# A top-2 mixture of experts behind a gated mLSTM block: seven half-size products for the first expert layer

## The chip, the cores and the metric

The kernel runs on one core of one Trainium2 chip. The metric is the time of one execution on the device in microseconds (us). Three runs of the kernel before gave 1991.71, 1995.03 and 1996.44 us, a median of 1995.03 us. The engines are named as the profile names them: PE (TensorE, the matrix products), DVE (VectorE), ACT (ScalarE), POOL (GpSimd) and SP (the queue that issues plain DMAs).

## The reference, cut to what matters

The program first computes a gated mLSTM attention block over 4096 tokens of width 512, then a feed-forward block of eight experts with two experts for each token. The change touches only the second:

```python
# x: 4096 tokens of width 512; E = 8 experts, K = 2, hidden width H = 2048
gates = softmax(xf @ Wg.T)                # router
topw, topi = top_k(gates, K)
C = int(round(K * T * 1.05 / E))          # 1075 slots an expert
buf = zeros((E, C + 1, D)).at[e_ord, pos].add(x_disp)[:, :C]
h = gelu(einsum('ecd,edh->ech', buf, W1) + b1, approximate=False)
y = einsum('ech,ehd->ecd', h, W2) + b2
out = einsum('tk,tkd->td', cw, y_tk)      # weighted by the router, added to x
```

## The kernel before

The program has two stages. The first 384 us (attention, router, ranks, and the table `slot_row` that says which token sits in which slot of which expert) are nearly untouched by the change. The rest is the stage of the experts.

An expert has `HI = 9` row tiles of `RT = 120` slots, 1080 in all. They are worked in `NC = 3` chunks of 360 slots. For each chunk, the hidden width of 2048 goes in `HT = 16` tiles of 128, so an expert has 48 steps. One step is `first_layer(n + 2)` followed by `second_layer(n)`:

- `first_layer` (L879) makes one hidden tile, 128 x 360, in one of three PSUM banks. The contraction over 512 has four parts. Each part has three products, because every operand is split into a rounded upper part and its rest (`w_hi` x `x_hi`, `w_hi` x `x_lo`, `w_lo` x `x_hi`). That is 12 matmuls with 360 moving columns.
- ACT takes Gelu of it twice (L1135 to `h_raw`, L1136 rounded to `h_hi`), DVE subtracts (L1495, `h_lo`).
- `second_layer` (L892) adds this hidden tile into the three output tiles of the chunk, 120 x 512 each, three products a tile: 9 matmuls with 512 moving columns. An output tile lives in its bank for 16 steps, so PSUM sums the whole hidden width.

After a chunk, DVE adds `b2` (L1511), scales by the router's weight (L1523), and POOL adds the 120 rows to `out` in DRAM by one indirect DMA (L603). There are 9 such adds for an expert, each waiting for the one before. POOL also gathers the token rows of the next chunk (L594) and the router's weights (L609). PE transposes the gathered rows (L862), ACT rounds them (L1060) and DVE makes the rest (L1480). The weights of an expert are split into `w_hi` and `w_lo` (L1070, L1071, L1451, L1453) in the last chunk of the expert before, and stay in place for the whole expert. Each engine has its own program in a fixed order. They meet at semaphores only.

Of the kernel before, what the change touches and what calls it, by code (L numbers as in the profile page):

```python
# [29 lines left out]
NH = 4  # L30
# [12 lines left out]
CT = 3  # L43
NC = HI // CT
CW = CT * RT
assert HI == CT * NC and CW <= 512 and CAP <= HI * RT
PAD = P
# [31 lines left out]
def build(nc, x, ctx_in, g_xattn, g_ffn, w_ig, b_ig, w_fg, b_fg, ln_w, w_router, w1, b1, w2, b2, out):  # L79
# [9 lines left out]
    with stack:  # L89
# [15 lines left out]
        slot_prob = sb("slot_prob", [P, NC, CT, E])  # L105
# [13 lines left out]
        pad_row = sb("pad_row", [P, 1], F32, a_mem)  # L119
        work = sb("work", [P, 2, TT // 2, E], F32, a_mem)  # L120
# [54 lines left out]
        x_hi = sb("x_hi", [P, NC, KT, CW], F32R)  # L175
        x_lo = sb("x_lo", [P, NC, KT, CW], F32R)
        h_raw = sb("h_raw", [P, 3, CW])
        h_hi = sb("h_hi", [P, 3, CW], F32R)
        h_lo = sb("h_lo", [P, 3, CW], F32R)
        y_out = sb("y_out", [P, CT, D])  # L180
# [3 lines left out]
        rows_add = [sb(f"rows_add{t}", [P, 1], I32) for t in range(CT)]  # L184
        rows_turn = sb("rows_turn", [P, HI], I32)
        w_hi = sb("w_hi", [P, HT, 2 * D], F32R)
        w_lo = sb("w_lo", [P, HT, 2 * D], F32R)

        raw = sb("raw", [P, 2, 4 * D])
        gathered = sb("gathered", [P, 3, D])  # L190
# [62 lines left out]
        prob_in = [sem(f"prob_in{c}") for c in range(NC)]  # L253
# [7 lines left out]
        raw_in = [sem(f"raw_in{i}") for i in range(2)]  # L261
        w_upper = sem("w_upper")
        w_ready = sem("w_ready")
        row_in = [sem(f"row_in{i}") for i in range(3)]
        rows_turned = sem("rows_turned")
        x_upper = sem("x_upper")
        x_ready = sem("x_ready")
        h_summed = sem("h_summed")
        h_upper = sem("h_upper")
        h_split = sem("h_split")  # L270
        y_step = sem("y_step")
        y_tile = sem("y_tile")
        y_taken = sem("y_taken")
        y_ready = sem("y_ready")
        y_added = sem("y_added")
        rows_free = sem("rows_free")
        b2_in = sem("b2_in")
        turn_rows_copied = sem("turn_rows_copied")
        b1_copied = sem("b1_copied")
# [3 lines left out]
        N_CONST = 9  # L283

# [42 lines left out]
        EARLY, SOON, LATER = range(0, 2), range(2, 4), range(4, HT)  # L327
# [18 lines left out]
        YB, HB, XB = 0, 3, 6  # L346

        STEPS = NC * HT


        TURN_AT = {c * HT + 7 + 2 * t: CT * c + t for c in range(NC) for t in range(CT)}


        AHEAD = 2

        def turns_of(n, last):
            m = TURN_AT.get(n)
            return [] if m is None or (last and m >= HI - CT) else [m]

        def x_place(m):  # L360

            return (m // CT + 1) % NC, m % CT
# [4 lines left out]
        from_start = [rows_free, y_taken, y_ready, x1_made, xn_made, *x1_stored, back_turned, back_copied, logits_made, logits_copied]  # L367
# [19 lines left out]
        def wait_step(eng, e, n):  # L387

            c, j = divmod(n, HT)
            if j == HT - 1:  # L390
                eng.wait_ge(y_tile, e * HI + CT * (c + 1))
            else:
                eng.wait_ge(y_step, e * (NC * (HT - 1)) + (c * (HT - 1) + j + 1))

        def w_at(j):

            return HT - 1 - j

# [10 lines left out]
        def _(sp):  # L409
# [62 lines left out]
            sp.dma_start(xn_dram[TOK:TOK + PAD, :], zeros[:, :]).then_inc(xn_stored, 16)  # L472
            sp.dma_start(out[TOK:TOK + PAD, :], zeros[:, :]).then_inc(pad_stored, 16)
            sp.dma_start(prob_dram[TOK:TOK + PAD, :], zeros[:, 0:E]).then_inc(prob_stored, 16)
# [9 lines left out]
            def load_weights(e, g, wait):  # L484

                if wait is not None:
                    wait_apart(sp, w_ready, wait)
                sp.dma_start(raw[:, g % 2, 0:2 * D].rearrange("p (k c) -> p k c", k=KT),
                             w1[e].rearrange("(k p) n -> p k n", p=P)[:, :, 2 * g * P:(2 * g + 2) * P]).then_inc(raw_in[g % 2], 16)
                sp.dma_start(raw[:, g % 2, 2 * D:4 * D].rearrange("p (j n) -> p j n", j=2),  # L490
                             w2[e, 2 * g * P:(2 * g + 2) * P, :].rearrange("(j p) n -> p j n", p=P)).then_inc(raw_in[g % 2], 16)
# [4 lines left out]
            for g in range(HT // 2):  # L496
                if g == 2:
                    store_x1(LAST_BATCH)
                    store_xn(LAST_BATCH)
                load_weights(0, g, None if g < 2 else 2 * (g - 1))  # L500
                if g == 3:
                    sp.wait_ge(prob_made, 1)
                    sp.dma_start(prob_dram[0:TOK, :].rearrange("(t p) e -> p t e", p=P), logits[:, :, :]).then_inc(prob_stored, 16)

            def load_b2(e):

                wait_apart(sp, y_taken, START + e * HI)
                sp.dma_start(b2_row[:, :], b2[e].partition_broadcast(P)).then_inc(b2_in, 16)

            with sp.Fori(0, E - 1) as e:  # L510
                load_b2(e)
                for g in range(HT // 2):
                    load_weights(e + 1, g, e * HT + (HT + 2 * (g - 1)))
            load_b2(E - 1)
            sp.wait_ge(y_added, 16 * HI * E)
            for p in range(2):
                sp.wait_ge(x1_stored[p], START + 16 * (B // 2))
            sp.wait_ge(pad_stored, 16)
# [6 lines left out]
        def _(pool):  # L525
# [9 lines left out]
            for p in range(2):  # L535
# [13 lines left out]
                   channel_multiplier=1, allow_small_or_imprecise_dtypes=True)  # L549
            G.iota(pad_row[:, :], pattern=[[0, 1]], base=TOK, channel_multiplier=1,  # L550
# [23 lines left out]
            def first_rests(tiles):  # L574

                for j in tiles:
                    pool.wait_ge(w_upper, j + 1)
                    G.tensor_tensor(w_lo[:, w_at(j), 0:D].rearrange("p (k c) -> p k c", k=KT), raw_w1(j),
                                    w_hi[:, w_at(j), 0:D].bitcast(F32).rearrange("p (k c) -> p k c", k=KT), ALU.subtract)
                    G.tensor_tensor(w_lo[:, w_at(j), D:2 * D], raw_w2(j), w_hi[:, w_at(j), D:2 * D].bitcast(F32), ALU.subtract)\  # L580
                        .then_inc(w_ready, 1)

# [4 lines left out]
            pool.wait_ge(pad_stored, 16)  # L587
# [10 lines left out]
            def add_rows(e, u, ordered=True):  # L598

                wait_apart(pool, y_ready, START + e * HI + (u + 1))  # L600
                if u > 0 and ordered:
                    wait_apart(pool, y_added, e * (16 * HI) + 16 * u)
                G.indirect_dma_start(out=out[:, :], out_offset=bass.IndirectOffsetOnAxis(ap=rows_add[u % CT][0:RT, :], axis=0),  # L603
                                     in_=y_out[0:RT, u % CT, :], in_offset=None, compute_op=ALU.add,
                                     bounds_check=TOK + PAD - 1, oob_is_err=True).then_inc(y_added, 16)
# [968 lines left out]
```

## Time and profile before

| | |
|---|---|
| median of three runs | 1995.03 us |
| the profiled execution | 1997.23 us |
| its span, first to last instruction | 1995.2 us |
| PE busy | 1899.8 us (95%) |
| DVE busy, ACT busy, POOL busy | 752.3 us, 790.7 us, 344.1 us |
| first matmul of an expert | 383.98 us |
| last matmul ends | 1981.4 us |
| moved by DMA | 158.10 MB |

The busy time of an engine is a union: matmuls overlap in the pipeline, so the mean duration of one (328 ns for 360 columns) is not its share of the time. That share is the distance between starts, which the chain and the timeline give.

### The profile page before, as it was taken

What the parts mean: (1) busy time and instruction counts of PE and PEld (TensorE: products, weight loads), DVE (VectorE), ACT (ScalarE), POOL (GpSimd) and SP (SyncE); (2) the same over time, 40 slices, a digit from 0 to 9 for tenths busy, and PEclk for the clock granted to TensorE, in tenths of its full rate; (3) what the DMA queues carried; (4) which work ended last, traced back from release to release, by engine and by line L of the source; (5) the groups of instructions that cost most, each with busy time, mean ns of one, the idle gap of its engine ahead of it and who ended that gap; (6) DMA issues with size and microseconds to landing.
All of it is one profiled execution on the core that took longest, in us unless ns stands there. A gap on an engine that the chain in (4) does not pass through costs nothing.

```text
span 1995.2 us, 28698 instructions
## 1 busy us (share of the span) xinstructions
PE 1899.8 (95%) x10268; PEld 1655.8 (83%) x10268; DVE 752.3 (38%) x1827; ACT 790.7 (40%) x1667; POOL 344.1 (17%) x302
## 2 busy tenths in 40 slices
PE   4999987799999999999999999999999999999997
PEld 3777766688888888888888888888888888888886
DVE  3589987412351235123512351235123512351221
ACT  2567667542352235223522352235223522352221
POOL 0001010262201220122012201220122012201200
PEclk8899987699999999999999999999999999999998
DMA  4255443331241123112311231123212321231111
GB/s 145 85 179 203 163 154 127 96 133 31 64 136 37 31 68 135 34 30 65 134 37 30 62 134 40 30 55 133 48 30 55 132 49 30 57 106 31 31 15 15
DMA packets 111349, 158.10 MB, mean 79 GB/s; under 512 B 13744, under 2 KB 63024, under 8 KB 110208
## 3 DMA queue, kind: packets, MB, share of 16 engines
q1 hardware_dynamic: 92800, 120.68, 18.0%
q0 software_dynamic: 18432, 35.69, 10.2%
q8 instruction: 95, 1.56, 0.3%
q14 instruction: 22, 0.18, 0.0%
HBM read 121.13 MB, written 35.20 MB: 78 GB/s over the span
## 4 chain that ended last, share of the span: by engine, by line
PE 84%; DMA 6%; DVE 4%; issue 3%; ACT 2%; SPq 1%; POOL 0%; POOLq 0%; DVEq 0%; ACTq 0%
PE PS L892 38%; PE PS L879 36%; DMA out_dram<-y_out,rows_add 3%; PE PS L731 3%; PE PS L722 2%; DMA vs<-in_ctx_dram 2%; PE PS L862 2%; PE PS L670 1%; PE PS L750 1%; ACT heads L976 1%; SPq L420 1%; DVE stats L1178 1%; PE PS L684 1%; DMA gathered<-xn_rows,rows_turn 1%; DVE decay L1236 0%
## 5 line engine op out<-in xcount | busy, mean ns | idle before, releaser
L1135 ACT ACTIVATE h_raw<-PS,b_now 128x360 f32<-128x360 f32 x384 | 215.5, 561 | 1035.9 <-PE PS L879 1033.9
L1495 DVE TENSOR_TENSOR h_lo<-h_raw,h_hi 128x360 fp32r<-128x360 f32 x384 | 205.2, 534 | 1074.5 <-ACT h_hi L1136 1073.6
L879 PE MATMUL PS<-x_hi,w_hi 128*128 128x360 f32 x1536 | 503.6, 328 | 2.7 <-issue 1.4
L879 PE MATMUL PS<-x_hi,w_lo 128*128 128x360 f32 x1536 | 503.5, 328 | 0.0
L879 PE MATMUL PS<-x_lo,w_hi 128*128 128x360 f32 x1536 | 501.9, 327 | 0.0
L892 PE MATMUL PS<-w_hi,h_hi 128*120 128x512 f32 x1152 | 459.9, 399 | 0.0
L892 PE MATMUL PS<-w_lo,h_hi 128*120 128x512 f32 x1152 | 453.9, 394 | 0.0
L892 PE MATMUL PS<-w_hi,h_lo 128*120 128x512 f32 x1152 | 453.2, 393 | 0.0
L603 POOL DMA_INDIRECT out_dram<-y_out,rows_add x72 | 129.1, 1793 | 1197.5 <-DVE y_out L1523 986.1
L879 PEld LDWEIGHTS PS<-x_hi,w_hi 128*128 128x128 f32 x1536 | 289.8, 189 | 25.0 <-issue 3.9
L879 PEld LDWEIGHTS PS<-x_lo,w_hi 128*128 128x128 f32 x1536 | 289.3, 188 | 16.4
L879 PEld LDWEIGHTS PS<-x_hi,w_lo 128*128 128x128 f32 x1536 | 289.9, 189 | 0.0
L892 PEld LDWEIGHTS PS<-w_hi,h_lo 128*120 128x120 f32 x1152 | 208.8, 181 | 59.1
L892 PEld LDWEIGHTS PS<-w_hi,h_hi 128*120 128x120 f32 x1152 | 209.2, 182 | 38.4
L892 PEld LDWEIGHTS PS<-w_lo,h_hi 128*120 128x120 f32 x1152 | 208.9, 181 | 38.3
L1136 ACT ACTIVATE h_hi<-PS,b_now 128x360 fp32r<-128x360 f32 x384 | 212.4, 553 | 0.0
L1451 DVE TENSOR_TENSOR w_lo<-raw,w_hi 128x512 fp32r<-128x512 f32 x114 | 78.8, 691 | 45.9 <-ACT w_hi L1071 45.9
L731 PEld LDWEIGHTS PS<-vs,decay 128*128 128x128 f32 x640 | 79.4, 200 | 8.4 <-issue 4.3
L731 PE MATMUL PS<-vs,decay 128*128 128x129 f32 x640 | 83.8, 288 | 0.7 <-DVE decay L1236 0.4
L1071 ACT CAST w_hi<-raw 128x512 fp32r<-128x512 f32 x128 | 80.2, 627 | 0.0
L1070 ACT CAST w_hi<-raw 128x512 fp32r<-128x512 f32 x128 | 79.6, 622 | 0.3
L1453 DVE TENSOR_TENSOR w_lo<-raw,w_hi 128x512 fp32r<-128x512 f32 x114 | 78.1, 685 | 0.0
(177 smaller groups left out, 1432.5 us busy)
## 6 DMA issues: line engine op xcount, KB each, us to landing
raw<-in_L_ffn_W_dram SPq DMA_DIRECT2D x128, 512.0 KB, 4.5
x_front<-in_x_dram SPq DMA_DIRECT2D x8, 1024.0 KB, 7.1
vs<-in_ctx_dram SPq DMA_DIRECT2D x32, 256.0 KB, 4.7
maxima<-maxima_rows SPq DMA_DIRECT2D x8, 1024.0 KB, 4.7
x_back<-in_x_dram SPq DMA_DIRECT2D x8, 1024.0 KB, 8.9
out_dram<-x_back SPq DMA_DIRECT2D x8, 1024.0 KB, 6.9
xn_rows<-xn SPq DMA_DIRECT2D x8, 1024.0 KB, 9.5
b_row<-in_L_ffn_b_dram SPq DMA_DIRECT2D x8, 256.0 KB, 3.6
```

The source lines that it names most:

```text
L603: G.indirect_dma_start(out=out[:, :], out_offset=bass.IndirectOffsetOnAxis(ap=rows_add[u % CT][0:RT, :], axis=0), in_=y_out[0:RT, u % CT, ...
L722: T.matmul(score_ps[t], kT[p][:, h, t * P:(t + 1) * P], qT[p][:, h, t * P:S], start=True, stop=True).then_inc(scores_made, 1)
L731: ins = T.matmul(head_ps[:, s, 0:DH + 1], decay[h % 2][:, t, s * P:(s + 1) * P], vs[p][:, t, h, 0:DH + 1], start=(t == 0), stop=(t == s))
L879: ins = T.matmul(PS[:, HB + n % 3, 0:CW], w[:, w_at(j), k * P:(k + 1) * P], v[:, c, k, :], start=(k == 0 and a == 0), stop=(k == KT - 1 an ...
L892: ins = T.matmul(PS[0:RT, YB + t, :], h[:, n % 3, t * RT:(t + 1) * RT], w[:, w_at(j), D:2 * D], start=(j == 0 and a == 0), stop=(j == HT - ...
L1070: A.copy(w_hi[:, w_at(j), 0:D].rearrange("p (k c) -> p k c", k=KT), raw_w1(j))
L1071: A.copy(w_hi[:, w_at(j), D:2 * D], raw_w2(j)).then_inc(w_upper, 1)
L1135: A.activation(h_raw[:, n % 3, :], PS[:, HB + n % 3, 0:CW], ACT.Gelu, bias=b1_now[:, n % HT:n % HT + 1])
L1136: A.activation(h_hi[:, n % 3, :], PS[:, HB + n % 3, 0:CW], ACT.Gelu, bias=b1_now[:, n % HT:n % HT + 1]).then_inc(h_upper, 1)
L1451: V.tensor_tensor(w_lo[:, w_at(j), 0:D].rearrange("p (k c) -> p k c", k=KT), raw_w1(j), w_hi[:, w_at(j), 0:D].bitcast(F32).rearrange("p (k ...
L1453: V.tensor_tensor(w_lo[:, w_at(j), D:2 * D], raw_w2(j), w_hi[:, w_at(j), D:2 * D].bitcast(F32), ALU.subtract)\
L1495: V.tensor_tensor(h_lo[:, n % 3, :], h_raw[:, n % 3, :], h_hi[:, n % 3, :].bitcast(F32), ALU.subtract)\
```

## The change

The first layer is computed by Winograd's form of Strassen's scheme, on halves. The contraction of 512 is cut in two halves of 256, two hidden tiles of 128 form a pair, and the slots are cut in quarters of `CW = 270`, two of which form a side (540 slots). One `2 x 2` block product then takes seven half-size products instead of eight. An expert has 8 pairs and 2 sides, so 16 blocks (`k` in the code). A block has seven products of 6 matmuls each (2 contraction parts x 3 rests) with 270 moving columns. The operands of the products are sums of weight quarters (`sum_w1`, four DVE operations for a pair) and of token quarters (`sum_x`, four for a side). The results of the seven products, in a ring of four PSUM banks, are combined by one ACT copy and seven DVE adds into `c_top` and `c_rows` in SBUF. Gelu reads them there.

The second layer now runs in groups of four hidden tiles. An output tile is finished after 4 tiles x 3 products = 12 matmuls, taken out, scaled and added to `out` in DRAM. So an expert has 36 adds instead of 9 (288 instead of 72 in all), `y_out` is a ring of three, and an add waits for nothing but its rows. `b2` is added only to the first nine tiles (`base_rows`, DVE). ACT scales all (`scale_rows`). The second layer lags the first by 20 tile steps (`LAG`), across experts.

Unrounded operands and their rests now share one place in SBUF (`same_place`). Weights come in rings of four pairs and are split during the expert, and the pads behind `out` triple.

```diff
-CT = 3
-NC = HI // CT
-CW = CT * RT
+CW = HI * RT // 4
+PAIRS = HT // 2
+RINGS = 3
+PAD = RINGS * P
...
+        PRODUCTS = ((A11, B11), (S2, T2), (S3, T3), (S1, T1), (A22, T4), (S4, B22), (A12, B21))
+        M1, M6, M7, M5, M4, M3, M2 = range(7)
+        U2, U3, C22, U4, C21, C12, C11 = range(1, 8)
+        USED_UP_BY = {M6: U2, M7: U3, M5: U4, M4: C21, M3: C12, M2: C11}
+        LAG = 20
+        def items(k):
+            q = 9 * k - LAG
+            return [[(q + i) for i in range(a, z)] for a, z in ((0, 2), (2, 4), (4, 6), (6, 9))]
+        def scaled_in(k):
+            u = 9 * (k // 4)
+            return ([u - 6, u - 5], [u - 4, u - 3], [u - 2, u - 1], [u, u + 1, u + 2])[k % 4]
...
# POOL
+            def add_rows(e, u):
+                wait_apart(pool, y_ready, e * NY + (u + 1))
+                G.indirect_dma_start(out=out[:, :], ... compute_op=ALU.add, ...).then_inc(y_added[u % RINGS], 16)
...
+                for k in range(BLOCKS):
+                    for u in scaled_in(k):
+                        if not (first and u < 0):
+                            add_rows(e, u)
...
+                    if k == 3 and not last:
...
+                        gather_side(e + 1, 0, rows_turn, True)
+                        wait_apart(pool, weight_copied, e + 1)
+                        gather_prob(rows_turn)
+                    if k == 14 and not last:
+                        gather_side(e + 1, 1, rows_turn, True)
...
# PE
-                for k in range(KT):
-                    for a, (w, v) in enumerate(((w_hi, x_hi), (w_hi, x_lo), (w_lo, x_hi))):
-                        ins = T.matmul(PS[:, HB + n % 3, 0:CW], w[:, w_at(j), k * P:(k + 1) * P], v[:, c, k, :],
+                for kt in range(2):
+                    for n, (w, v) in enumerate(((w1_hi, x_hi), (w1_hi, x_lo), (w1_lo, x_hi))):
+                        ins = T.matmul(product_at(k, i), w[:, slot, a, kt * P:(kt + 1) * P], v[:, side, x, kt, :],
...
+            def second_layer(e, q):
+                g, t, i = q // 36, q % 36 // 4, q % 4
+                u = HI * g + t
...
+                    before = u - 2
+                    if 0 <= before < HI:
+                        pe.wait_ge(y_based, e * HI + (before + 1))
+                    else:
+                        wait_past(pe, y_ready, e * NY + (before + 1))
...
+                    product(e, k, M1)
+                    product(e, k, M6)
+                    rows(0)
+                    rest(0)
+                    rows(1)
+                    product(e, k, M7)
+                    product(e, k, M5)
+                    rows(2)
+                    rest(1)
+                    product(e, k, M4)
+                    rows(3)
+                    rest(2)
+                    rows(4)
+                    product(e, k, M3)
+                    product(e, k, M2)
+                    rest(3)
...
# DVE
+            def base_rows(e, u):
+                dve.wait_ge(y_tile, e * NY + (u + 1))
...
+                wait_past(dve, y_added[u % RINGS], e * (16 * NY // RINGS) + 16 * (u // RINGS))
+                V.tensor_tensor(y_out[0:RT, u % RINGS, :], PS[0:RT, YB + u % 2, :], b2_row[0:RT, :], ALU.add).then_inc(y_based, 1)
```

On PE, at the border between a step's second layer and the next first layer, the order before is this (`h_split` counts the rests that DVE made, `h_upper` the tiles that ACT rounded):

```order
L892 MATMUL PS<-w_hi,h_hi 120x512 [waits h_split]
L892 MATMUL PS<-w_lo,h_hi 120x512
L892 MATMUL PS<-w_hi,h_lo 120x512
...
L879 MATMUL PS<-x_hi,w_hi 128x360 [waits h_upper]
L879 MATMUL PS<-x_lo,w_hi 128x360
L879 MATMUL PS<-x_hi,w_lo 128x360
```

In the changed program, PE at the end of block `k = 5` of an expert, the last product and then the item that closes tile 7 and the one that opens tile 8 (`c_made` counts the DVE adds that empty a bank, `y_based` the output tiles with `b2`):

```order
L958 MATMUL PS<-x_hi,w1_hi 128x270 [waits c_made]
L958 MATMUL PS<-x_lo,w1_hi 128x270
L958 MATMUL PS<-x_hi,w1_lo 128x270
...
L980 MATMUL PS<-w2_hi,h_hi 120x512
L980 MATMUL PS<-w2_lo,h_hi 120x512
L980 MATMUL PS<-w2_hi,h_lo 120x512
L975 REGISTER_ALU
L980 MATMUL PS<-w2_hi,h_hi 120x512 [waits y_based]
```

Each product is a shorter run of matmuls behind a wait of its own, and an output tile opens behind a wait for the tile two before it.

On POOL, an expert of the loop before: the adds stand three at a time, each behind the one before, with three gathers and three weight gathers between:

```order
L594 DMA gathered<-xn_rows,rows_turn 120x512 [waits rows_turned] x3
L609 DMA slot_prob<-prob_rows,rows_turn 120x8 x3
L384 REGISTER_ALU
L384 REGISTER_ALU [waits y_ready]
L603 DMA out_0_dram<-y_out,rows_add0 4224x512 [waits y_added]
```

And in the changed program, block `k = 3` of an expert and the first add of block 4:

```order
L674 DMA out_0_dram<-y_out,rows_now 4480x512 [waits y_ready]
L430 ISA
L430 ISA [waits row_in0,row_in1,row_in2,row_in3,row_in4]
L706 ISA [waits prob_in]
L706 COPY rows_turn<-slot_row 128x9
...
L663 DMA gathered<-xn_rows,rows_turn 120x512 [waits rows_turned] x2
L681 DMA slot_prob<-prob_rows,rows_turn 120x8 [waits weight_copied]
L681 DMA slot_prob<-prob_rows,rows_turn 120x8 x8
L430 REGISTER_ALU
L674 DMA out_0_dram<-y_out,rows_now 4480x512 [waits y_ready]
```

Five row gathers and nine weight gathers of the next expert now stand in one run between two adds.

On DVE, in block `k = 5`, the base of tile 6 stands between two steps of the combination:

```order
L1717 TENSOR_TENSOR c_top<-PS,c_top 128x270 [waits product_made]
L1665 REGISTER_ALU
L1666 REGISTER_ALU [waits w1_summed]
L1667 TENSOR_TENSOR w1_lo<-w1_raw,w1_hi 128x512 [waits w1_upper]
L1708 REGISTER_ALU
L423 REGISTER_ALU [waits y_tile]
L1712 TENSOR_TENSOR y_out<-PS,b2_row 120x512 [waits y_added0]
L1716 REGISTER_ALU
L1717 TENSOR_TENSOR c_rows<-PS,c_rows 128x270 [waits product_made]
```

What DVE had free of waits on DRAM now has a wait for an add (`y_added0`) in the midst of it.

## Rows read from the trace of the kernel before

**Rows 1.** The page: busy time, share of the span, instructions.
```profile
PE 1899.8 (95%) x10268; PEld 1655.8 (83%) x10268; DVE 752.3 (38%) x1827; ACT 790.7 (40%) x1667; POOL 344.1 (17%) x302
```

**Rows 2.** The chain that ended last, near its end: start us, us, what.
```profile
1950.76 2.09 PE PS L892 x9
...
1973.14 1.98 PE PS L879 x12
1975.12 6.28 PE PS L892 x27
```

**Rows 3.** Stretches: us, busy and count of PE, PEld, DVE, ACT, POOL; PEclk, DMA, GB/s.
```profile
200.00:206.00 6.00, 6.00 (x44) 4.77 (x41) 5.19 (x16) 5.37 (x14) 0.29 (x1) 1.00 0.00 0
384.00:390.00 6.00, 6.00 (x22) 6.00 (x23) 0.00 (x0) 1.96 (x3) 3.63 (x5) 0.55 0.77 232
440.00:640.00 200.00, 199.82 (x1051) 177.60 (x1050) 61.95 (x120) 69.95 (x140) 43.76 (x36) 1.00 0.28 72
1220.00:1241.00 21.00, 20.51 (x111) 18.24 (x112) 4.36 (x8) 5.51 (x11) 3.15 (x4) 1.00 0.08 22
```

**Rows 4.** Timeline of PE and its weight loads in the attention stage: start, us.
```profile
202.56 0.75 PEld L700 LDWEIGHTS PS<-g_log,ones 128*128 128x128 f32 x6
204.27 1.95 PE L731 MATMUL PS<-vs,decay 128*128 128x129 f32 x16
```

**Rows 5.** Groups of the page: busy us, mean ns of one, idle before.
```profile
L1495 DVE TENSOR_TENSOR h_lo<-h_raw,h_hi 128x360 fp32r<-128x360 f32 x384 | 205.2, 534 | 1074.5 <-ACT h_hi L1136 1073.6
L1451 DVE TENSOR_TENSOR w_lo<-raw,w_hi 128x512 fp32r<-128x512 f32 x114 | 78.8, 691 | 45.9 <-ACT w_hi L1071 45.9
L731 PE MATMUL PS<-vs,decay 128*128 128x129 f32 x640 | 83.8, 288 | 0.7 <-DVE decay L1236 0.4
```

**Rows 6.** Timeline of DVE and ACT in the expert stage.
```profile
559.99 0.69 DVE L1451 TENSOR_TENSOR w_lo<-raw,w_hi 128x512 fp32r<-128x512 f32 x1 [0.49 <-ACT w_hi L1071]
560.60 0.69 DVE L1453 TENSOR_TENSOR w_lo<-raw,w_hi 128x512 fp32r<-128x512 f32 x1
...
566.45 0.56 ACT L1135 ACTIVATE h_raw<-PS,b_now 128x360 f32<-128x360 f32 x1 [1.97 <-PE PS L879]
566.91 0.55 ACT L1136 ACTIVATE h_hi<-PS,b_now 128x360 fp32r<-128x360 f32 x1
567.35 0.62 ACT L1070 CAST w_hi<-raw 128x512 fp32r<-128x512 f32 x1
```

**Rows 7.** Timeline of POOL, the border of two experts.
```profile
808.27 1.92 POOL L603 DMA_INDIRECT out_dram<-y_out,rows_add  x1 [4.07 <-DMA out_dram<-y_out,rows_add]
814.49 0.19 POOL L623 COPY rows_turn<-slot_row 128x9 int32 x1 [4.30 <-issue]
815.80 1.05 POOL L594 DMA_INDIRECT gathered<-xn_rows,rows_turn  x1 [1.12 <-issue]
...
822.33 0.98 POOL L609 DMA_INDIRECT slot_prob<-prob_rows,rows_turn  x1 [0.31 <-issue]
```

**Rows 8.** The adds of 790 to 1020 us: durations, times from issue to landing.
```profile
L603 POOL DMA_INDIRECT out_dram<-y_out,rows_add x12: 1584/1686/2937, 792.7 to 1008.1; - x12
DMA to landing us min/median/max: 4.8/5.1/8.9
```

**Rows 9.** Timeline of PE at the first matmuls of the experts, and after an idle time.
```profile
385.05 0.50 PE L879 MATMUL PS<-x_hi,w_hi 128*128 128x360 f32 x1
385.35 0.50 PE L879 MATMUL PS<-x_lo,w_hi 128*128 128x360 f32 x1
...
1220.49 0.60 PE L862 MATMUL PS<-ident,gathered 120*128 120x120 f32 x4 [1.69 <-DMA gathered<-xn_rows,rows_turn]
```

**Rows 10.** The chain at the start of the experts: start us, us, what.
```profile
377.40 4.13 DMA gathered<-xn_rows,slot_row
...
381.58 1.08 PE PS L862 x4
...
383.98 8.60 PE PS L879 x36
```

**Rows 11.** The chain at the end.
```profile
1987.38 1.57 POOL out_dram L603
```

More of the change, by code:

```diff
@@ L343, in there @@
             return not isinstance(b[0], int) or 0 <= b[1] < B
[L346 to L362, printed above, removed]
+        MB, YB, XB = 0, 4, 6
+        B11, B21, T1, B22, T3, T2, T4 = range(7)
@@ L519, in _ @@
+            expert(0, True, False)
+            with sp.Fori(1, E - 1) as e:
+                expert(e, False, False)
+            expert(E - 1, False, True)
+            for r in range(RINGS):
+                sp.wait_ge(y_added[r], 16 * NY // RINGS * E)
+            for p in range(2):
+                sp.wait_ge(x1_stored[p], START + 16 * (B // 2))
+            sp.wait_ge(pad_stored, 16 * N_PAD)
             sp.wait_ge(xn_stored, 16 * (B + 1))
@@ L642, in _, with gather_side @@
-            expert(0, False, first=True)
+            def gather_side(e, side, rows, wait):
+                for s, t in enumerate(TURNED[side]):
+                    gather(rows[:, t:t + 1], s, e * 10 + (5 * side - 5 + s + 1) if wait else None)
+            def add_rows(e, u):
+                wait_apart(pool, y_ready, e * NY + (u + 1))
+                G.indirect_dma_start(out=out[:, :], out_offset=bass.IndirectOffsetOnAxis(ap=rows_now[0:RT, u % HI:u % HI + 1], axis=0),
+                                     in_=y_out[0:RT, u % RINGS, :], in_offset=None, compute_op=ALU.add,
+                                     bounds_check=TOK + PAD - 1, oob_is_err=True).then_inc(y_added[u % RINGS], 16)
@@ new lines, in expert, with rows, rest @@
+            def expert(e, first, last):
+                for k in range(BLOCKS):
+                    mine = [[q for q in part if not (first and q < 0)] for part in items(k)]
+                    turn = (e, 1) if k == 0 else (e + 1, 0) if k == 14 and not last else None
+                    def rows(s):
+                        if turn is not None:
+                            turn_rows(*turn, s)
+                    def rest(part):
+                        for q in mine[part]:
+                            second_layer(e, q)
+                    product(e, k, M1)
[14 more added lines that the diff above has]
+                    rest(3)
@@ L913, in _ @@
+            expert(0, True, False)
+            with pe.Fori(1, E - 1) as e:
+                expert(e, False, False)
+            expert(E - 1, False, True)
+            for q in range(9 * BLOCKS - LAG, 9 * BLOCKS):
+                second_layer(E - 1, q)
         @block.scalar
```

689 lines of the change are left out of this document (420 added, 269 removed).

## The prediction

> **What bounds the kernel now.** I read the busy times first: PE is busy 95% of the span, DVE 38%, ACT 40%, POOL 17% [rows 1]. An average hides stages, so next the stretches: in 440 to 640 us PE is busy 199.82 of 200 us at clock 1.00 (the 2.4 GHz level) [rows 3]. Then the chain: from 1950.76 to 1975.12 it is nothing but L892 and L879 in turn, six pairs in 24.36 us, 4.060 us a pair [rows 2]. So the experts are bound by PE, and only what PE streams, or what makes PE wait, can move the time.
>
> Unit prices on PE. Twelve 360-column matmuls take 1.975 us, 164.6 ns each. The nine of 512 columns take 4.060 - 1.975 = 2.085, 231.7 ns each [rows 2]. The line through both is 0.4414 ns a column plus 5.7 ns. The old stage in these prices: 4608 x 0.1646 + 3456 x 0.2317 = 758.5 + 800.7 = 1559.2 us, and 69 turns of token rows of four transposes, which start and end within 0.60 us, the last one's latency of some 0.19 included [rows 9], so 0.41 us each, 28.3. Sum 1587.5, against 1981.4 - 384.0 = 1597.4 measured [rows 2, 10]. The 9.9 us left are 2.4 of a cold start (18 matmuls at 300 ns, clock 0.55 [rows 3, 9]) and 7.5 of small idles at the experts' borders.
>
> **What the change removes from PE.** 4608 matmuls of 360 columns become 16 blocks x 7 products x 6 x 8 experts = 5376 of 270. No row shows 270 columns with these operands. The line gives 0.4414 x 270 + 5.7 = 124.9 ns. Below, I take 270 columns at the 2.4 GHz level, 112.5 ns, plus the 3.5 ns that L731 leaves: its sixteen records take 1.95 us, the last 0.288 long, so they are 111 ns apart [rows 4, 5], against 107.5 for 129 columns streamed twice (an estimate, as fp32 operands need more than one pass). That gives 116. Above, 112.5 plus the whole excess of the 512-column matmul (231.7 - 213.3 = 18.4) is 131. The weight load could be the new limit, since it must fit under a shorter matmul. But six loads of 128 columns go by in 0.75 us behind matmuls of 12 columns, (0.75 - 0.19) / 5 = 112 ns apart [rows 4], and L731 reaches 111 ns with a load for each record. So loads fit, barely. I take 124.9, the line through the two nearest rows: 5376 x 0.1249 = 671.5 us, 87.0 us less than now. Ends: 623.6 and 704.3.
>
> The trace's 164.6 ns stands 14.6 over 150.0. The Trainium skill (TensorE: Matmul & The Clock Gate, Back-to-back issue gap) gives N / 2.4 + 2.5 ns, which would be 152.5 here. The trace disagrees by 12 ns, the measurement decides, and by the page the product matmuls would take 115.0 ns, 618 us in all.
>
> The second layer keeps its 3456 matmuls: 800.7 us. Turns go from 9 to 10 an expert (one tile straddles both sides): 75 x 0.41 = 30.8 us after the first matmul. Other idles stay at 7.5.
>
> **What it adds on DVE and ACT.** Two 512-column subtractions start 0.61 us apart, and durations grow from 534 ns at 360 columns to 691 at 512, 1.033 ns a column [rows 5, 6]. So 270 columns occupy DVE for 0.36 us (result after 0.44) and 540 for 0.64 (after 0.72). Per expert: 112 adds x 0.36 = 40, 32 splits of Gelu x 0.64 = 20, sums and splits of weights 37, of tokens 14, nine bases 5.5: about 117 us. ACT: 64 Gelus of 540 (0.46 apart at 360 [rows 6], in proportion 0.69) = 44, casts 512 wide at about 0.52 for 30, 36 scalings at 0.6 = 22, the rest 17: about 113. An expert takes PE 112 x 6 x 0.1249 + 432 x 0.2317 + 4.1 = 188.1 us, so both engines hide (62%, 60%). POOL: 36 adds x 1.7 and 19 gathers x 1.3, 86 us [rows 7, 8]. The 216 more adds move 245 KB each, 53 MB on top of 158, with the DMA engines at 0.28 now [rows 3]. The throughputs hold; the order is what can hurt.
>
> A block is 7 x 0.75 + 9 x 0.695 = 11.5 us on PE. I laid the waits out by hand. M1 and M6 end at 1.5, M5 at 4.4, M4 at 6.5, M2 at 9.4. The combination needs a bank only one to four products later, 4 us of slack. The tight chain is M2's result 9.65, its DVE add 10.1, both Gelus 11.45, rest 12.1 us, wanted by PE at 13.0 in every fourth block. Where the token turns stand (blocks 15 and 0) the rest comes 0.7 late, and the opening of tile 2 waits 0.7 for a base (L1712). I charge 1.5 us an expert, 12 us; ends 0 and 30.
>
> **The wait that replaces a free run.** Before, POOL's adds were the slow part but nothing on PE depended on them soon. Now `base_rows(6)` in block 5 waits on DVE until add 3 has landed, and PE opens tile 8 at the end of block 5 only after `base_rows(6)`. Counting from the start of block 3: add 2 is issued at about 10 and ends at 11.5. Then POOL runs six waits and the copy (about 1.5), 1.1 us to the first gather, and fourteen gathers 1.29 us apart (18.1) [rows 7]. Add 3 is issued at 32.6, lands 4.9 later at 37.5 (4.8 to 5.1 is usual [rows 8]), and the base ends at 38.3. PE reaches tile 8 at 3 x 11.5 - 1.4 + 0.7 = 33.8. So PE stands 4.5 us, once in each of the seven experts that gather for a next one: 31.5 us. Behind the waiting base on DVE stand C21, C12, C11 and a split. They catch up within block 6, since PE stands as well. Ends: 0 (POOL 4.5 us quicker) and 60 (landing 8.9).
>
> **Start and end.** The start needs five row tiles instead of three, 2 x 1.3 us of gathers, and four chained DVE sums, 2.8, before a product: first matmul at 390 instead of 384.0 [rows 7, 10]. Then DVE still has seven token splits (4.5) and the second pair's sums and splits (3.8) in front of the first add of block 0, and blocks 0 and 1 have no second layer to fill PE. I place the point from which PE is full 17 us behind its work (some cold matmuls, at 300 ns for 360 columns [rows 9], included); ends 8 and 28. The end is shorter: before, 13.8 us from the last matmul to the end of the span, with three adds behind it, the last issued at 1987.38 [rows 11]. Now one tile remains: scaling 0.65, issue and landing 5.1, the same 2.9 after landing, 8.7 in all.
>
> **Sum.** 390 + 671.5 + 800.7 + 30.8 + 7.5 + 12 + 31.5 + 17 = 1961.0, plus 8.7 is a span of 1969.7 us against 1995.2. The execution lasts 2.0 us longer than its span, 1971.7 against 1997.23, and the median before lies 2.2 below the profiled execution, so 1969.5 in the median's terms; I forecast 1969 us.
>
> **Rivals.**
> - *No gap at the gathers.* POOL ends its gathers in time, or DVE is not that early. For it: 4.5 us of some 38 is within what I can place by hand. Then 31.5 us fall away: 1938 us; with products at 116 ns, 1890.
> - *The add lands late* (the slower side). The place is the same DVE base in block 5. The first add after a pause landed after 8.9 us instead of 5.1, with an issue of 2.9 [rows 8], and PE's clock may fall behind the idle time. If so the gap is 4.5 + 3.8, and 2.4 us of cold matmuls follow (18 x 135 ns [rows 9]): 10.7 x 7 = 75 instead of 31.5, 2013 us. It is slower than before from 8.2 us a gap on. Against it: in my layout no weight load is under way there. Idle of 1.69 us left the clock at 1.00 [rows 3, 9], and no row shows one of 4.5 behind a full-speed stretch. The Trainium skill (the page named above, HAM oscillation) has waits between bursts of matmuls drop the clock; by it this rival gains.
> - *The weight load binds.* If load and matmul add up a little at 270 columns, 131 ns: 33 us more, 2002 us. It eats the gain from 129.7 ns on. Against it, L731's 111 ns.
> - *The chains are late in every block*, at least 0.2 us in each of 128: 25 us and more, 1995 or above. It would show as PE waiting for DVE at `h_split` or `c_made`. For it: a wait for each product where there were two for 21 matmuls.
>
> **Chances.** Forecast, with gaps of 1 to 8 us an expert: 0.47, of which 0.42 is faster. No gap: 0.25. Late landing: 0.11. Load binds: 0.09, half of it still no slower. Chains late: 0.08. A difference under 0.2% (4 us) can't be told from none in this kernel. That gives faster 0.70, same 0.08, slower 0.22. Range for 8 in 10: 1925 to 2005. The likeliest case alone: 1950 to 1990.
>
> **What would show it.** Right: L958 (the products) about 125 ns apart at clock 1.00; PE idle once an expert for some 4.5 us in front of L980 behind DVE's L1712, which itself waits for the DMA of `out_dram`; POOL with 14 gathers in a row; DVE and ACT near 60% busy in the stage. Wrong: spacings of 116 or 131; no such idle; PE idle at L958 behind `c_made` in every block; first product well off 390.

## The result and the profile after

The changed kernel takes 2036.9 us in the median of four runs (2034.05 to 2041.72), the kernel before 1995.7 in four runs beside them. The ratio is 1.021, with a 95% interval of 1.018 to 1.024: slower by 2.1%, clear of the noise, and outside the range of 1925 to 2005. The profiled execution has a span of 2032.3 us.

The profile's page of the changed kernel: busy times (for [rows 1]), the queue of the DMAs that POOL issues, and a group of matmuls (for [rows 5]). The profile leaves the numbers out of names, so `w_hi` there can be `w1_hi` or `w2_hi`, and `b_row` is `b2_row`:

```profile
PE 1859.9 (92%) x11068; PEld 1597.8 (79%) x11068; DVE 1277.3 (63%) x2881; ACT 1108.0 (55%) x2035; POOL 677.1 (33%) x506
...
q0 software_dynamic: 50176, 90.77, 30.4%
...
L958 PE MATMUL PS<-x_hi,w_hi 128*128 128x270 f32 x1792 | 525.6, 293 | 24.4 <-issue 13.2
```

PE works 40 us less than before and yet the kernel ends 37 us later, so PE stands or runs at its lower clock. Stretches (us, busy and count of PE, PEld, DVE, ACT, POOL; PEclk, DMA, GB/s) show where; the columns are those of [rows 3]:

```profile
440.00:640.00 200.00, 196.31 (x1176) 172.51 (x1175) 127.68 (x253) 109.27 (x186) 85.18 (x61) 0.99 0.56 107
1081.00:1174.00 93.00, 93.00 (x559) 82.23 (x558) 58.26 (x119) 50.03 (x81) 30.98 (x19) 1.00 0.53 97
```

In the middle of an expert PE is never idle. The chain of waits there (start us, us, what; for [rows 2]) has the same piece in every block:

```profile
1081.53 2.10 PE PS L980 x9
...
1127.61 2.10 PE PS L980 x9
```

Four blocks in 46.08 us, 11.52 each. Of that the 27 matmuls of 512 columns take 6.26 at the old price of 231.7 ns, so 42 of 270 columns take 5.26, 125.3 ns each. The products cost what was forecast.

The loss is at two places of each expert. ACT's copy `c_first` opens every block, so the distance of its 128 records gives the length of each block. The means over experts 1 to 5 in us, worked out from the timelines of ACT in four kernels (the last three are experiments below; quiet blocks are 11.5 in all):

```
block                          0     1     2     3     4     5     6    14    15   expert
changed kernel              19.8  10.3  10.2  12.2  22.8  11.8  11.5  14.2  13.2   204 to 208
spread gathers              19.4  10.3  10.2  12.2  13.0  10.1  11.5  13.9  13.0   192 to 196
late add, no extra gathers  19.4  10.3  10.2  12.2  12.5  16.0  11.9  14.2  13.4   198 to 202
spread and written out      17.0  10.1  10.4  12.3  12.3  10.7  11.5  13.6  11.5   190.1
```

Blocks 4 and 5 hold 34.6 us where 23.0 would do, and the border (15 and 0) 33.0 where 28.5 would do. Expert 0, which stands ahead of the loop, loses less: 28.5 us in blocks 4 and 5.

**Place one, blocks 4 and 5.** POOL in expert 3 of the changed kernel (start, us), the counterpart of [rows 7]:

```profile
1048.80 0.76 POOL L706 COPY rows_turn<-slot_row 128x9 int32 x1
1050.67 1.04 POOL L663 DMA_INDIRECT gathered<-xn_rows,rows_turn  x1 [1.11 <-issue]
...
1067.60 0.98 POOL L681 DMA_INDIRECT slot_prob<-prob_rows,rows_turn  x1 [0.30 <-issue]
1068.89 1.64 POOL L674 DMA_INDIRECT out_dram<-y_out,rows_now  x1 [0.30 <-issue]
```

Fourteen gathers, 18.2 us, then add 3: as forecast. What DVE, ACT and PE do meanwhile was not:

```profile
1059.19 0.44 DVE L1717 TENSOR_TENSOR c_top<-PS,c_top 128x270 f32<-128x270 f32 x1 [0.87 <-PE PS L958]
1063.48 0.44 DVE L1717 TENSOR_TENSOR c_top<-PS,c_first 128x270 f32<-128x270 f32 x1 [3.85 <-remote]
...
1073.40 0.44 DVE L1717 TENSOR_TENSOR c_top<-PS,c_first 128x270 f32<-128x270 f32 x1 [7.01 <-remote]
1073.76 0.68 DVE L1712 TENSOR_TENSOR y_out<-PS,b_row 120x512 f32<-120x512 f32 x1
```
```profile
1072.63 0.39 ACT L1270 COPY c_first<-PS 128x270 f32<-128x270 f32 x1 [7.29 <-remote]
```
```profile
1060.84 0.29 PE L958 MATMUL PS<-x_hi,w_lo 128*128 128x270 f32 x1
...
1063.98 0.39 PE L958 MATMUL PS<-x_hi,w_hi 128*128 128x270 f32 x1
1064.92 0.29 PE L958 MATMUL PS<-x_lo,w_hi 128*128 128x270 f32 x1 [0.55 <-issue]
1065.63 0.28 PE L958 MATMUL PS<-x_hi,w_lo 128*128 128x270 f32 x1 [0.43 <-issue]
...
1074.49 0.78 PE L980 MATMUL PS<-w_hi,h_hi 128*120 128x512 f32 x1 [2.68 <-DVE y_out L1712]
```

By its records PE ends M1 of block 5 at about 1061.1, and ACT, which waits for nothing else, copies it at 1072.63: the signal is 11.5 us late. M3's sum on DVE is at 1059.19 and M2's at 1063.48, 4.3 us for six matmuls, 0.7 us each instead of 0.125; from then on PE's own records come in steps of 0.7 us too, with "issue" as the cause. From M2's sum to M1's copy lie 15 more matmuls in 9.2 us, 0.6 us each, so it is PE that is slow and not a single signal that is late. It is some five times slower from about 1059 on, while hardly a DMA runs (the first stretch below: 3 GB/s) and PE waits for nobody. That the ends of PE's records don't show it agrees with the Trainium skill (Perfetto Trace Analysis, Summary: the profiler window per engine type), by which the end of a TensorE record is an estimate; the readers of a result are the better clock.

Does PE wait for its own instructions? The DMA records of 1053 to 1082 us have this line alone, and none of an instruction queue, though PE runs steadily again from 1074.49:

```profile
q0 software_dynamic: 1095, 1.91, 35.9%
```

The base at 1073.76 is not the one of the prediction. It is `base_rows(5)`, the first of block 5 in DVE's order. It needs add 2, which was issued at 1047.36 and had long landed, and it is late only because DVE waited for PE; PE's 2.68 us in front of tile 7 come from that. `base_rows(6)` follows at 1077.67, 8.8 us after add 3 was issued, without a wait for it, and PE opens tile 8 at 1082.07 without an idle time. So it is in all of experts 1 to 6. Over the whole kernel DVE's bases wait for an add once, for 0.6 us (us, times):

```profile
  DMA out_dram<-y_out,rows_now: 0.6, 1
```

That once is in expert 0. Elsewhere the predicted wait does not occur in the changed kernel: PE comes so late that add 3 has landed. Some 2.5 of the 11.6 us that the two blocks lose are the lower clock, which starts near 1070, when the matmuls are already slow: the fifteen matmuls from 1074.49 to 1079.83 take 5.3 us where their usual prices give 2.8. The stretches:

```profile
1061.00:1064.00 3.00, 3.00 (x21) 2.53 (x19) 0.52 (x2) 0.04 (x1) 2.27 (x3) 1.00 0.05 3
...
1070.00:1075.00 5.00, 1.50 (x3) 0.75 (x3) 1.60 (x4) 0.91 (x2) 2.14 (x2) 0.50 0.73 95
1075.00:1080.00 5.00, 5.00 (x17) 4.08 (x16) 4.14 (x10) 3.57 (x7) 1.60 (x1) 0.51 0.36 42
```

**Place two, the border of two experts.** DVE and PE at the end of expert 1:

```profile
786.30 1.35 DVE L1696 TENSOR_TENSOR x_lo<-x_raw,x_hi 128x540 fp32r<-128x540 f32 x2 [1.35 <-ACT x_hi L1232]
791.59 0.72 DVE L1703 TENSOR_TENSOR h_lo<-h_raw,h_hi 128x540 fp32r<-128x540 f32 x1 [3.94 <-issue]
```
```profile
792.45 0.49 PE L980 MATMUL PS<-w_hi,h_hi 128*120 128x512 f32 x1 [3.33 <-DVE h_lo L1703]
```

DVE jumps back to the top of its loop (L1801) and does nothing for 3.9 us; no semaphore is named. The same stand is at all five borders from expert 2 to 6 (3.4 to 4.0 us), and PE idles 1.9 to 3.3 us behind it. The DMA records of 784 to 794 us hold five packets of instructions:

```profile
q14 instruction: 4, 0.03, 0.9%
q8 instruction: 1, 0.02, 0.6%
```

The rest of block 15's C11 (L1703) is the first thing behind the jump, and PE's first tile of block 0 wants it at once.

### The profile page after: what moved, and what is told of

Same layout as the page of the kernel before. It is cut to its first block, busy times and chain, and to the rows that moved or that the text cites. A ratio compares the mean times of both kernels' runs of the same rounds, so it can differ in the third digit from the quotient of the medians.

```text
span 2032.3 us, 34102 instructions
## 1 busy us (share of the span) xinstructions
PE 1859.9 (92%) x11068; PEld 1597.8 (79%) x11068; DVE 1277.3 (63%) x2881; ACT 1108.0 (55%) x2035; POOL 677.1 (33%) x506
## 4 chain that ended last, share of the span: by engine, by line
PE 80%; DVE 6%; issue 4%; ACT 3%; DMA 3%; another core or an unknown queue 3%; SPq 1%; POOL 0%; DVEq 0%; POOLq 0%; ACTq 0%
PE PS L980 37%; PE PS L958 31%; PE PS L805 3%; DMA vs<-in_ctx_dram 2%; PE PS L796 2%; PE PS L936 2%; PE PS L744 1%; PE PS L869 1%; SPq L452 1%; PE PS L824 1%; PE PS L758 1%; DVE h_lo L1703 1%; ACT heads L1087 1%; DVE y_out L1712 1%
## 5 line engine op out<-in xcount | busy, mean ns | idle before, releaser
L674 POOL DMA_INDIRECT out_dram<-y_out,rows_now x288 | 485.7, 1686 | 928.5 <-ACT y_out L1283 802.7
L958 PE MATMUL PS<-x_hi,w_hi 128*128 128x270 f32 x1792 | 525.6, 293 | 24.4 <-issue 13.2
L958 PE MATMUL PS<-x_lo,w_hi 128*128 128x270 f32 x1792 | 521.9, 291 | 8.8 <-issue 8.4
L958 PE MATMUL PS<-x_hi,w_lo 128*128 128x270 f32 x1792 | 520.7, 291 | 8.3 <-issue 8.1
L980 PE MATMUL PS<-w_hi,h_hi 128*120 128x512 f32 x1152 | 466.0, 405 | 39.8 <-DVE y_out L1712 18.6
L980 PE MATMUL PS<-w_hi,h_lo 128*120 128x512 f32 x1152 | 458.8, 398 | 0.8 <-issue 0.8
L980 PE MATMUL PS<-w_lo,h_hi 128*120 128x512 f32 x1152 | 459.1, 399 | 0.2 <-issue 0.2
L980 PEld LDWEIGHTS PS<-w_hi,h_hi 128*120 128x120 f32 x1152 | 212.0, 184 | 86.5 <-DVE y_out L1712 27.2
L980 PEld LDWEIGHTS PS<-w_hi,h_lo 128*120 128x120 f32 x1152 | 212.0, 184 | 61.3 <-issue 1.5
L980 PEld LDWEIGHTS PS<-w_lo,h_hi 128*120 128x120 f32 x1152 | 212.4, 184 | 32.2 <-issue 0.9
L1717 DVE TENSOR_TENSOR c_top<-PS,c_first 128x270 f32<-128x270 f32 x256 | 112.0, 438 | 177.8 <-PE PS L958 113.2
L1703 DVE TENSOR_TENSOR h_lo<-h_raw,h_hi 128x540 fp32r<-128x540 f32 x256 | 183.4, 716 | 36.6 <-issue 18.7
L1283 ACT ACTIVATE y_out<-PS,weight_now 120x512 f32<-120x512 f32 x216 | 148.6, 688 | 89.2 <-PE PS L980 88.7
L1717 DVE TENSOR_TENSOR c_rows<-PS,c_rows 128x270 f32<-128x270 f32 x256 | 112.0, 438 | 86.6 <-PE PS L958 78.1
L1667 DVE TENSOR_TENSOR w_lo<-w_raw,w_hi 128x512 fp32r<-128x512 f32 (+1 forms) x192 | 147.8, 772 | 0.1
L1240 ACT CAST w_hi<-w_raw 128x512 fp32r<-128x512 f32 (+1 forms) x192 | 127.6, 688 | 33.5 <-DVE w_raw L1655 24.3
```

Of the source, the lines that this page charges most:

```text
L958: ins = T.matmul(product_at(k, i), w[:, slot, a, kt * P:(kt + 1) * P], v[:, side, x, kt, :], start=(kt == 0 and n == 0), stop=(kt == 1 and ...
L980: ins = T.matmul(PS[0:RT, YB + u % 2, :], tile_of_h(h, i, t), w[:, pair % 4, j, :], start=(i == 0 and n == 0), stop=(i == 3 and n == 2))
L1240: A.copy(w1_hi[:, p % 4, a:z, :], w1_raw[:, p % 4, a:z, :]).then_inc(w1_upper, 1)
L1283: A.activation(mine, src, ACT.Copy, scale=weight_now[0:RT, u % HI:u % HI + 1]).then_inc(y_ready, 1)
L1667: ins = V.tensor_tensor(w1_lo[:, p % 4, a:z, :], w1_raw[:, p % 4, a:z, :], w1_hi[:, p % 4, a:z, :].bitcast(F32), ALU.subtract)
L1703: V.tensor_tensor(h_lo[:, 2 * (k % 2) + row, halves, :], h_raw[:, 2 * (k % 2) + row, halves, :], h_hi[:, 2 * (k % 2) + row, halves, :].bit ...
```

## The experiments

Each version has its own line numbers: L981 and L986 are L980 here, L1704 is L1703, and L1713 and L1718, where they write `y_out`, are L1712. All ratios are to the kernel before, run beside the version; gains and losses between versions are differences of medians.

**1. Spread the probability gathers.** The run of 14 becomes 5, 3, 3 and 3.

```diff
                         gather_side(e + 1, 0, rows_turn, True)
                         wait_apart(pool, weight_copied, e + 1)
-                        gather_prob(rows_turn)
+                    if k in (5, 7, 9) and not last:
+                        gather_prob(rows_turn, range(3 * (k - 5) // 2, 3 * (k - 5) // 2 + 3))
```

> The nine probability gathers of the next expert, which POOL issued in one run behind the five row gathers in block 3, are issued in threes behind the adds of blocks 5, 7 and 9; nothing else changes. Theory B (POOL's run of 14 gathers is what disturbs blocks 4 and 5 of each expert, either because add 3 stands behind it or because the run slows the other engines' signals): the stalls of DVE (3.8 us at L1717) and ACT (7 to 8 us at L1270), the matmuls 0.7 us apart and the slow clock after them go; about 12 us an expert, 7 experts, so the time falls by 60 to 90 us, to 1950 to 1975. Rival (the stall belongs to the place in the loop, an instruction fetch of DVE, ACT or PE, and POOL only happens to be busy then): the same stall stays in blocks 4 and 5, and the time stays at 2030 to 2040.

Measured: 1959.7 us (1958.1 to 1959.9), ratio to the kernel before 0.981 [0.980, 0.983]. The stall goes from all experts (row two of the table), 77 us in the 7 experts that gather, 11.0 each. The rival, the place in the loop, falls.

**2. One probability gather instead of nine,** in the same place (edit: `gather_prob(rows_turn, range(1))`, and waits for 16 instead of 144).

> POOL issues one probability gather of the nine in the loop (the other eight are left out, so experts 1 to 7 scale tiles 1 to 8 by weights gathered for expert 0); the one stands where the nine stood. Theory B: as with the spread gathers, 60 to 90 us less, and if the run of gathers disturbs by its number, nothing is left of the stalls in blocks 4 and 5. Rival (place in the loop): 2030 to 2040.

Measured: 1964.8 us, 0.984 [0.983, 0.986]. Six gathers in a run cost next to nothing, 5 us in all; the place alone is not the cause.

**3. Write out the loop over experts,** on all engines, on DVE alone, on PE alone.

```diff
-            with dve.Fori(1, E - 1) as e:
+            for e in range(1, E - 1):
```

> The loop over experts 1 to 6 is written out on all five engines (constants instead of registers, no backward branch); order of the work and the run of 14 gathers stay. Theory A (DVE stands 3.3 to 3.9 us at its backward branch once an expert, now on the chain that PE waits for): the gap of about 3.3 us on PE before block 0 of experts 2 to 6 and the slow clock behind it go, 5 to 6 us a border, so 25 to 40 us less: 1997 to 2012. If the stall in blocks 4 and 5 were instruction fetch tied to the loop as well, it goes too and the time is about 1950. Rival (branch costs nothing, the stand is DVE waiting for something else): 2030 to 2040.

> Only DVE's loop over experts is written out. Theory A: the same gain as with all engines written out, within 5 us, if DVE's branch is the only one on the chain. Rival: PE's or ACT's branch stands next behind it, and less than half of the gain comes.

> Only PE's loop over experts is written out; the run of 14 gathers stays. With all engines written out the stall in blocks 4 and 5 shrank from about 12 us to 3 or 4 us an expert in experts 1 to 5, with DVE alone it didn't. Theory: it is PE's own instructions in the loop (waits against registers, refetch) that make the run of gathers costly, so most of the 52 us less 22 us of DVE come here: 2005 to 2010. Rival (POOL's or SP's or ACT's loop does it, or the exact time at which the run falls): 2030 to 2037.

Measured: all 1985.0 (0.995 [0.993, 0.996]); DVE 2015.1 (1.010 [1.008, 1.011]); PE 2047.7 (1.027 [1.024, 1.030]). DVE alone brings 22 us, and the gap before block 0 is gone from its trace: place two is DVE's jump, and no other engine's stands next behind it. With all written out, place one shrinks too (blocks 4 and 5 of experts 1 to 5 hold 28.5 us instead of 34.6 in its profiled execution), which neither PE's loop nor DVE's alone does: with PE's alone the kernel is 11 us slower than the changed one. It isn't the loop as such either, since expert 0 of the changed kernel has 28.5 as well, and expert 6 has 33.0 with everything written out. That part of my theory for the third run is wrong, and what in the layout of the program makes the stall of place one longer or shorter I could not settle.

**4. Both remedies.**

> Both remedies: probability gathers in threes behind blocks 5, 7 and 9, and the loop over experts written out on all engines. If stalls A (DVE's branch, 22 us over five borders) and B are separate, the gains add: 1960 less 22 to 28, so 1932 to 1940. If they share a cause, 1950 or more.

Measured: 1937.4 us (1936.1 to 1938.7), 0.9715 [0.970, 0.973]. The gains of 77 and 22 us add up, so the two places are separate. This version beats both kernels. PE (the stretch of [rows 3], and at the border):

```profile
440.00:640.00 200.00, 198.99 (x1205) 175.70 (x1205) 130.35 (x258) 112.60 (x191) 89.30 (x65) 1.00 0.57 111
```
```profile
774.28 0.50 PE L981 MATMUL PS<-w_hi,h_hi 128*120 128x512 f32 x1 [0.50 <-DVE h_lo L1704]
```

**5. How long a run?** Nine probability gathers behind the adds of block 7; then five row and four probability gathers in block 3 and five in block 7.

> The nine probability gathers stay one run, but stand behind the adds of block 7 instead of behind the five row gathers in block 3. Theory B1 (the slow stretch of PE comes from the length of a run of gathers on POOL, here 9, before 14): the stretch of matmuls 0.7 us apart moves to blocks 7 and 8 and is shorter than with 14, or is gone; between the changed kernel's 2037 and the spread gathers' 1960. If only runs longer than about 10 disturb: 1960 to 1970. If the probability gathers themselves disturb, however few stand before them: a stall of 5 us or more an expert near blocks 7 to 9, 1990 or more. Rival (only the place beside block 4 matters): 1955 to 1965, with no slow stretch anywhere.

> In block 3 stand the five row gathers and four probability gathers in one run (9), in block 7 the other five. If the length of the run decides: as with the run of nine in block 7, 20 to 25 us above the spread version: 1978 to 1986, with a slow stretch of PE about 8 us behind the start of the run. If nine probability gathers are what disturbs and row gathers don't count: 1960 to 1965. If any gathers in block 3 beyond five cost as much each: 1985 to 2000.

Measured: 1982.8 (0.995 [0.993, 0.997]) and 1982.8 us (0.995 [0.993, 0.996]). A run of nine costs 23 us, 3.3 an expert, at both places and with either mix of tables; it shows in blocks 8 and 9 (17.0 + 8.5) and in blocks 4 and 5 (16.9 + 9.6), 23.0 being the usual sum. By length: six 0.7 us an expert, nine 3.3, fourteen 11.0.

**6. The late add without the gathers.** On the spread version, POOL copies a spare tile behind the five row gathers, each copy waiting for the one before:

```diff
+                        for t in range(24):
+                            G.tensor_copy(spare[:, :], ident[:, :]).then_inc(spare_made, 1)
+                            wait_apart(pool, spare_made, e * 24 + (t + 1))
```

> The spread version (probability gathers in threes behind blocks 5, 7, 9) with 12 small memsets of a spare tile put on POOL where the nine gathers stood, some 8 to 12 us of POOL's time without a DMA. Theory P (the prediction's step: add 3 stands behind POOL's run, base_rows(6) and then tile 8 wait for it): add 3 is as late as before, so about 1 to 4.5 us an expert come back: 1967 to 1990, with PE waiting once an expert for y_out of L1713 and no matmuls 0.7 us apart. Theory B (it is the gathers themselves that make PE slow): the late add alone costs little, 1960 to 1970. If POOL's time alone does it all: 2030.

> The memsets of the last such run took POOL only 0.6 us, so it did not test the late add. Here the spread version gets seven copies of a 128x128 tile into a spare one on POOL behind the five row gathers of block 3, each waiting for the one before, some 8 to 13 us of POOL without a DMA. Theory P (the prediction's step: add 3 late by as much, base_rows(6) and then PE wait): PE waits once an expert for y_out of L1713 for 1 to 5 us and the time is 1967 to 1995. Theory B (the gathers themselves slow PE, the late add is mostly covered): 1958 to 1966, no matmuls 0.7 us apart.

Measured: 1959.7 and 1958.4 us, no change. Twelve memsets took POOL 0.61 us and seven copies 5 us, too little to test it; the second at least shows that add 3 has 5 us of slack.

> The seven copies of the last such run took POOL 0.46 us each, so add 3 was only 5 us later and nothing waited for it. Here they are 24, some 11 to 12 us of POOL without a DMA, as long as the nine gathers that stood there. Theory P (the late add, as the prediction had it): PE waits once an expert 2 to 5 us for y_out of L1713: 1975 to 1995. Theory B (late add covered): 1957 to 1966. Against the changed kernel's 2037 either leaves the rest to the gathers themselves.

> As the last one with 19 copies instead of 24, which puts add 3 about 18.2 us behind the first gather, where the changed kernel has it. If the late add were all of the changed kernel's loss against the spread version (77 us), this gives 2030 to 2037. If the gathers themselves take part (the row of block times has 10 us more in block 4 with them, none without): PE idle once an expert for about 4 us behind y_out, 6 to 7 us an expert with the slow clock, 2000 to 2010, and the 27 to 37 us between are the gathers' own.

Measured: 2024.6 us with 24 copies (add 3 issued 20.5 us behind the first gather), 2002.5 (1998.2 to 2005.8; 1.004 [1.002, 1.005]) with 19 (18.2 us, as in the changed kernel: 1036.48 to 1054.72). This is the mechanism that the prediction described, and only in these two versions does it show in full (with all loops written out, experiment 3, DVE waits for add 3 too, 3.6 us over the kernel). In expert 3 of the version with 19:

```profile
1054.72 1.65 POOL L676 DMA_INDIRECT out_dram<-y_out,rows_now  x1 [1.16 <-issue]
```
```profile
1059.41 0.69 DVE L1718 TENSOR_TENSOR y_out<-PS,b_row 120x512 f32<-120x512 f32 x1 [6.01 <-DMA out_dram<-y_out,rows_now]
```
```profile
1060.16 0.49 PE L986 MATMUL PS<-w_hi,h_hi 128*120 128x512 f32 x1 [3.82 <-DVE y_out L1718]
```

DVE's `base_rows(6)` waits for the DMA of add 3 and PE waits 3.8 us for DVE in front of tile 8. No matmuls stand 0.7 apart, though POOL works all the time, and block 4 has its normal length. Over the kernel DVE's bases now wait for an add seven times, for 41.2 us, against once and 0.6 us in the changed kernel (us, times):

```profile
  DMA out_dram<-y_out,rows_now: 41.2, 7
```

It costs 42.8 us, 6.1 an expert. PE's idle is 3.8 to 4.1 us in experts 1 to 6 (1.8 in expert 0); the rest, some 2.3, comes behind it, most of it by the lower clock (the columns as above):

```profile
1061.60:1064.90 3.30, 3.30 (x15) 3.09 (x15) 2.61 (x5) 2.13 (x4) 2.62 (x2) 0.50 0.66 89
```

Five copies more, 2.3 us later, cost 3.2 an expert more.

**7. The run of gathers without the late add.** All nine probability gathers behind the row gathers of block 14, where no `base_rows` is near:

```diff
-                        gather_prob(rows_turn)
                     if k == 14 and not last:
                         gather_side(e + 1, 1, rows_turn, True)
+                        gather_prob(rows_turn)
```

> The nine probability gathers stand behind the five row gathers of block 14, a run of 14 again, where no base_rows is near. If a run of 14 slows PE by itself: some 8 us behind its first gather, in block 15 or 0, one block is 5 to 10 us longer than in the spread version, with signals from PE late and matmuls 0.7 us apart, 1995 to 2030. If only the late add at base_rows costs: 1958 to 1970, unless the scaling on ACT waits for an add there (then seen as ACT waiting for the DMA of out_dram).

Measured: 2040.9 us (1.022 [1.019, 1.026]), 81 us above experiment 1, 11.6 an expert. Blocks 4 and 5 are normal (13.1 + 9.9), block 15 takes 23.9 instead of 13.0 and block 0 21.2. The first gather starts at 1173.52, and neither PE, whose matmuls come in steps of 1.4 us here, nor DVE waits for a DMA:

```profile
1193.68 0.59 PE L980 MATMUL PS<-w_hi,h_lo 128*120 128x512 f32 x1 [0.84 <-issue]
1195.09 0.58 PE L980 MATMUL PS<-w_hi,h_hi 128*120 128x512 f32 x1 [0.82 <-issue]
```
```profile
1196.57 0.44 DVE L1717 TENSOR_TENSOR c_rows<-PS,c_rows 128x270 f32<-128x270 f32 x1 [2.96 <-remote]
```

**8. The same run in the kernel before:** nine more gathers into a spare tile behind the six of the first third, so 15 in a row.

> The kernel before the change with nine more probability gathers into a spare tile behind the six gathers that POOL issues ahead of the first third's adds (a run of 15, once an expert for all eight experts); they serve nothing. Theory B (a long run of gathers on POOL slows PE by itself, whatever the kernel): matmuls 0.6 to 0.7 us apart and later signals from PE some 8 us into the run, 5 to 12 us an expert, 40 to 90 us more: 2035 to 2085. Rival (only the changed kernel's tight chain suffers, through late adds): 1995 to 2010, no slow stretch of matmuls.

Measured: 2035.6 us (1.020 [1.018, 1.023]), 41 us for nine gathers that nobody waits for, 5.2 an expert. The gathers start at 1032.91 there; ACT, which got its product at 1041.44, gets the next at 1053.42:

```profile
1041.89 0.56 ACT L1144 ACTIVATE h_hi<-PS,b_now 128x360 fp32r<-128x360 f32 x1
1053.42 0.56 ACT L1143 ACTIVATE h_raw<-PS,b_now 128x360 f32<-128x360 f32 x1 [10.97 <-remote]
```

So a long run of gathers on POOL slows PE in either kernel.

## Why the prediction was wrong

The sum was 1961.0 to the last matmul, measured 2022.6. Term by term:

- *Products and second layer*, 671.5 + 800.7: right. 128 blocks at 11.52 are 1474.6 against 1472.2, and 125.3 ns stand against the 124.9 of the line. Rival "the load binds" is out.
- *First product at 390*: 389.25. *End 8.7 us*: 2022.62 to 2032.3, 9.7.
- *Token turns, other idles, small stalls, ramp* (30.8 + 7.5 + 12 + 17 = 67.3): the version of experiment 4 has none of the two losses; from its first product at 389.4 to its last matmul at 1925.18 lie 1535.8 us, less 1474.6 leaves 61.2. Right within 6 us, though as a sum only: the four terms were not measured one by one, and the turns stand in blocks 14 and 0, not 15 and 0. Rival "chains late in every block" is out: nine of its sixteen blocks take 11.5 us.
- *The wait that replaces a free run*, 31.5 us: this step failed. It said that PE stands 4.5 us in each of seven experts in front of tile 8, behind `base_rows(6)` and add 3. In the changed kernel PE doesn't stand there at all in experts 1 to 6, and DVE's bases wait for an add once, for 0.6 us. The prediction counted the fourteen gathers as POOL's time only. The gathers slow PE itself from some 8 us into the run: 11.6 us an expert where no base is near (experiment 7), 11.0 in the changed kernel, where PE becomes so late that it covers the late add. So in place of 31.5 us stand 77, not within the ends of 0 and 60. The wait as such is real, and was sized nearly right: with other work for POOL in place of the gathers PE idles 3.8 to 4.1 us (experiment 6), and the prediction's own terms, 11.5 + 1.5 + 1.1 + 18.1, put add 3 at 32.2 and not at 32.6, a gap of 4.1. What it left out even of this wait is the clock behind it, some 2.3 us a gap; no row of before showed an idle time that long, and in experiment 6 the granted clock is 0.50, the 1.2 GHz level, right behind it. That agrees with the Trainium skill's rule (TensorE: Matmul & The Clock Gate, HAM oscillation), which the prediction had cited for its rival alone.
- *A term that was not in the sum*: DVE's jump at the end of its loop. The first rest behind it was counted as 0.7 late in block 0; that DVE would stand 3.4 to 4.0 us at the jump was not seen. It cost 22 us over the five borders.

Together 45.5 + 22 - 6 = 61.5, near the 62 us by which the span was missed. The slower rival came nearest to the time, and nearly hit the price (10.7 us a gap), by luck: its mechanism was an add that lands late, and add 3 landed 4.6 to 4.9 us after issue in experts 1 to 6. The rival "no gap at the gathers" named 1938 us. The changed kernel has no gap behind the add and is still slow, so that rival is wrong as well; with both losses removed the kernel runs in 1937.4.

What stays open is the way by which a run of gathers reaches PE. Shown are: from the seventh gather or so on, in both kernels, with more or fewer of either kind of gather, while the DMA engines have little to do. It is not POOL's work as such (24 copies in experiment 6 slow no matmul), and not instructions of PE that arrive late by DMA (no such packet in the slow stretch). Not shown is the resource that they share, and whether the number of gathers in a row or the time that they take decides: their pace was some 1.3 us in every run. Nor is it known why the stall is shorter with all loops written out (experiment 3).

## What to carry to other kernels

Issue indirect gathers on POOL in short groups (up to five or six here) between its other work, even where POOL and the DMA engines are idle enough: the run is paid by PE. When a change hangs PE's next step on an engine that used to have slack, look at what that engine does at its loop border, and keep the first instruction behind a backward jump off the tight chain or write the loop out. A queue's late item and the side effects of what stands ahead of it are two costs; put neutral work of the same length in its place to see the one alone.

## What the runs showed of the hardware

- A run of 9, 14 or 15 indirect gathers 1.29 us apart costs 3.3, 11.0 and 5.2 us an expert (the last in the kernel before). From some 8 us behind its first one, matmuls take about 0.7 us each in the changed kernel (270 columns, 0.125 us normally). PE's records at first don't show it, the "remote" waits of DVE and ACT for PE do.
- DVE stands 3.4 to 4.0 us at the backward jump of its loop over an expert, with packets of the instruction queues in the DMA records of that time. With the loop written out PE idles 0.5 us at that place instead of 1.9 to 3.3.
- A 270-column matmul with these operands and a weight load of its own takes 125.3 ns, 12.8 above its 112.5 ns at the 2.4 GHz level; 360 and 512 columns had 14.6 and 18.4.
